# Rope's turned half multiplied ahead of the rotation and summed in PSUM, with the order of a stage rearranged

## What is computed

```python
def _rope(t):
    t1, t2 = (t[..., :d // 2], t[..., d // 2:])
    rot = jnp.concatenate([-t2, t1], axis=-1)
    return t * cos + rot * sin
q = jax.nn.silu(x @ Wq); k = jax.nn.silu(x @ Wk); v = x @ Wv
q = _rope(q); k = _rope(k)
energy = jnp.einsum('bhnd,bhmd->bhnm', q, k) * mask
out = jnp.einsum('bhnm,bhmd->bhnd', energy, v)
```

## Time and profile before

| | |
|---|---|
| runs, us | 509.13, 513.08, 508.7 |
| median | 509.13 |
| the profiled execution, its own time | 512.64 |
| its span, first to last instruction | 510.7 |
| mean granted TensorE clock | 0.84 |
| busy in the span, PE / DVE / ACT / POOL | 367.9 / 267.4 / 204.7 / 290.5 |
| first energies of the stages 1 to 6 start at | 42.54, 72.84, 108.61, 141.52, 177.34, 207.56 |

### The profile page before, as it was taken

How to read it: one execution, slowest core, us unless ns; L and a number is a source line. 1 busy time by engine, 2 the same in 40 slices (tenths; PEclk the granted TensorE clock), 3 DMA queues, 4 the chain that set the end, 5 groups by cost and what they waited for, 6 DMA issues and landing times.

```text
span 510.7 us, 10114 instructions
## 1 busy us (share of the span) xinstructions
PE 367.9 (72%) x2456; PEld 301.0 (59%) x2457; DVE 267.4 (52%) x1094; ACT 204.7 (40%) x583; POOL 290.5 (57%) x205
## 2 busy tenths in 40 slices
PE   6586878998698776932218878989988989999000
PEld 4464756876576565722117656878877878878000
DVE  0344563877938858587205554444544444444035
ACT  1232052160240421402005656766767676766100
POOL 3000000038377085687865888888888888888523
PEclk9797877799967977555658999999999999999555
DMA  7999994003223753159546999999999989998894
GB/s 216 330 332 303 451 354 147 2 15 76 62 56 82 293 159 81 42 163 348 125 102 132 162 149 157 156 155 155 157 154 153 153 146 164 154 156 121 149 255 152
DMA packets 66303, 85.81 MB, mean 168 GB/s; under 512 B 16840, under 2 KB 61302, under 8 KB 65894
## 3 DMA queue, kind: packets, MB, share of 16 engines
q1 hardware_dynamic: 35734, 59.82, 37.5%
q0 software_dynamic: 29680, 24.95, 33.7%
q10 hardware_dynamic: 864, 0.73, 0.5%
HBM read 45.86 MB, written 39.47 MB: 167 GB/s over the span
## 4 chain that ended last, share of the span: by engine, by line
DVE 23%; PE 21%; issue 17%; DMA 15%; POOL 10%; ACT 8%; ACTq 3%; SPq 1%; DVEq 0%; POOLq 0%
DMA sums_d<-e_sb,tok 10%; POOL rows_d L376 7%; PE B L413 5%; PE B L658 3%; ACT UPW L803 3%; POOL sums_d L391 3%; PE B L667 3%; PE B L486 2%; DVE e_sb L977 2%; ACTq L269 2%; DMA W<-sums_d 2%; ACT e_sb L823 2%; DVE stats L846 2%; PE B L570 1%; DVE h L1143 1%
## 5 line engine op out<-in xcount | busy, mean ns | idle before, releaser
L391 POOL DMA_INDIRECT sums_d<-e_sb,tok x112 | 174.0, 1554 | 41.9 <-issue 24.4
L376 POOL DMA_INDIRECT rows_d<-xrow,slot x77 | 104.1, 1351 | 156.4 <-issue 126.9
L658 PEld LDWEIGHTS B<-e_sb,UPW 128*128 128x128 f32 x796 | 105.6, 193 | 10.9 <-issue 5.0
L658 PE MATMUL B<-e_sb,UPW 128*128 128x128 f32 x796 | 109.9, 279 | 0.1
L667 PE MATMUL B<-W,e_sb 128*128 x224 | 74.4, 414 | 21.4 <-DVE e_sb L1134 11.1
L1134 DVE TENSOR_TENSOR e_sb<-e_sb,B 128x128 f32<-128x128 f32 (+1 forms) x112 | 32.3, 288 | 84.2 <-ACT e_sb L811 47.9
L803 ACT COPY UPW<-W 128x512 f32 (+1 forms) x112 | 63.2, 564 | 18.7 <-issue 18.7
L646 PE MATMUL B<-ident,e_sb 128*128 128x128 f32 x224 | 44.1, 280 | 19.9 <-DMA e_sb<-rows_d 19.2
L1118 DVE COPY e_sb<-B 128x256 f32<-128x256 f32 x112 | 46.9, 419 | 19.0 <-PE B L646 18.2
L667 PEld LDWEIGHTS B<-W,e_sb 128*128 128x128 f32 x224 | 34.0, 191 | 35.9 <-issue 35.6
L823 ACT ACTIVATE e_sb<-B,wcol 128x256 f32<-128x256 f32 x112 | 53.0, 473 | 0.0
(11 more groups left out here) (160 smaller groups left out, 475.3 us busy)
## 6 DMA issues: line engine op xcount, KB each, us to landing
e_sb<-rows_d SPq DMA_DIRECT2D x112, 152.5 KB
rows_d<-padrow SPq DMA_DIRECT2D x1, 7320.0 KB, 33.6
W<-in_wx SPq DMA_DIRECT2D x1, 7027.0 KB, 50.3
sums_d<-padrow SPq DMA_DIRECT2D x4, 1408.0 KB, 21.7
W<-in_wx SPq DMA_DIRECT2D x1, 4781.0 KB, 16.6
W<-in_wx SPq DMA_DIRECT2D x1, 4576.0 KB
W<-in_pt SPq DMA_DIRECT2D x4, 666.0 KB, 6.9
sums_d<-e_sb,tok POOLq DMA_INDIRECT x112
```

The costliest lines, as they stand in the source:

```text
L376: pool.indirect_dma_start(rows_d, bass.IndirectOffsetOnAxis(ap=slot[0:n, t, j:j + 1], axis=0), xrow[0:n, t, :], None).then_inc(done, 16)
L391: pool.indirect_dma_start(sums_d[c], bass.IndirectOffsetOnAxis(ap=tok[:, c:c + 1], axis=0), Y[:, c, :], None, compute_op=ALU.add).then_inc ...
L658: mm = pe.matmul(B[2 + u % 2][:, m * P:(m + 1) * P], UPW[:, u % 2, at:at + P], GT[:, u % 2, k, :], start=k == 0, stop=k == KC - 1)
```

## The change

Rope takes another form. VectorE now makes two products from q and k: times the cosine (`rp`) and times the sine with its sign (`rs`, a new buffer of 888 columns). PE turns `rs` and adds `rp` to it in the same PSUM bank through a matmul with the identity. ScalarE splits q and copies k out of PSUM.

The order of a stage changes. On PE the second tile's energies come ahead of the shared projection and no longer behind an embedding, and wait for the masks strip by strip; the first half of the embedding goes behind the attends; the rank comes ahead of the second half; in the first stages the projection and `fold` go ahead of the embedding. On VectorE `place` stands ahead of the embedding's moments and the norms, no longer behind rope. The ranks use bank B[1]. GpSimd scatters the last block's anchors ahead of three of tile 9's choices.

Small instructions of VectorE on one tensor and two constants become `scalar_tensor_tensor` with a tensor of constants, and moments and additions of a block's two tiles go in pairs.

```diff
-            for b, tiles in enumerate(BLOCKS):
+            half = CHOICES // 2 + 1
+            for b, tiles in enumerate(BLOCKS[:-1]):
                 pool.wait_ge(slot_ok, b + 1)
                 for t in tiles:
                     scatter(t, [0], scat_anchor)
                 for t in tiles:
-                    scatter(t, range(1, CHOICES), scat)
+                    scatter(t, range(1, half if t == NT - 2 else CHOICES), scat)
+            pool.wait_ge(slot_ok, NB)
+            scatter(NT - 1, [0], scat_anchor)
+            for t in (NT - 2, NT - 1):
+                scatter(t, range(half if t == NT - 2 else 1, CHOICES), scat)
...
             def rotate(b):
                 n = SIZES[b]
+                pe.wait_ge(rope_ok, b + 1)
                 for half in range(2):
-                    pe.wait_ge(qk_ok, 2 * b + half + 1)
                     for c in range(KC):
-                        m = pe.matmul(B[4 + half][:, c * BT:c * BT + n], turn[:, :], qk[:, half * KC + c, 0:n],
-                                      start=True, stop=True)
+                        part = B[4 + half][:, c * BT:c * BT + n]
+                        pe.matmul(part, turn[:, :], rs[:, half * KC + c, 0:n], start=True, stop=False)
+                        m = pe.matmul(part, ident[:, :], rp[:, half * KC + c, 0:n], start=False, stop=True)
                     m.then_inc(rot_ps, 1)
...
             def second_transposes(b):
                 pe.wait_ge(x2_ok, BLOCKS[b][-1] + 1)
+                if b:
+                    pe.wait_ge(slot_ok, b)
...
             def split_heads(b):
-                act.wait_ge(rope_ok, b + 1)
+                n = SIZES[b]
+                act.wait_ge(rot_ps, 2 * b + 1)
                 for odd in range(2):
-                    m = act.activation(q_two[:, odd, :, 0:SIZES[b]], qk[:, 0:KC, 0:SIZES[b]], ACT.Copy,
-                                       scale=parity[:, odd:odd + 1])
-                m.then_inc(qh_ok, 1)
+                    act.activation(q_two[:, odd, :, 0:n], two_chunks(B[4], n), ACT.Copy, scale=parity[:, odd:odd + 1])
+                act.wait_ge(rot_ps, 2 * b + 2)
+                act.copy(qk[:, KC:2 * KC, 0:n], two_chunks(B[5], n)).then_inc(qh_ok, 1)
...
-                step(dve.tensor_scalar(g2, g1, 2.0, -BIG, ALU.is_ge, ALU.mult))
+                step(dve.scalar_tensor_tensor(g2, g1, 2.0, least[0:n, 0:GROUPS * k], ALU.is_ge, ALU.mult))
...
             def rope(b):
                 n = SIZES[b]
                 dve.wait_ge(qk_ok, 2 * b + 2)
-                q, shape = of_images(qk[:, :, 0:n], b, 2 * KC)
-                r, _ = of_images(rp[:, :, 0:n], b, 2 * KC)
-                step(dve.tensor_tensor(r, q, cossin[:, 0, :].unsqueeze(1).unsqueeze(1).to_broadcast(shape), ALU.mult))
+                x, shape = of_images(qk[:, :, 0:n], b, 2 * KC)
+                for dst, factor in ((rp, 0), (rs, 1)):
+                    y, _ = of_images(dst[:, :, 0:n], b, 2 * KC)
+                    m = dve.tensor_tensor(y, x, cossin[:, factor, :].unsqueeze(1).unsqueeze(1).to_broadcast(shape), ALU.mult)
+                m.then_inc(rope_ok, 1)
                 add_bias(b)
-                for half in range(2):
-                    dve.wait_ge(rot_ps, 2 * b + half + 1)
-                    turned = B[4 + half][:, 0:KC * BT].rearrange("p (c t) -> p c t", c=KC)[:, :, 0:n]
-                    x, shape = of_images(turned, b, KC)
-                    dst, _ = of_images(qk[:, half * KC:(half + 1) * KC, 0:n], b, KC)
-                    m = dve.tensor_tensor(dst, x, cossin[:, 1, :].unsqueeze(1).unsqueeze(1).to_broadcast(shape), ALU.mult)
-                step(m)
-                dve.tensor_tensor(qk[:, :, 0:n], qk[:, :, 0:n], rp[:, :, 0:n], ALU.add).then_inc(rope_ok, 1)
-                dve.wait_ge(rope_ok, b + 1)
...
                 if mid is not None:
                     attended(mid)
+                if last is not None:
+                    place(last)
                 if coming is not None:
                     embedded(coming)
```

More of the change, by code:

```diff
@@ L602, in _ @@
                     normed_transposes(ahead)
+                for t in tiles[1:]:
+                    energies(mid, t)
+                if mid is not None:
+                    attend(mid, tiles[0])
                 if last is not None:
                     shared_up(last)
+                for t in tiles[1:]:
+                    attend(mid, t)
+                if ahead == 0:
+                    pe.wait_ge(ld["rest"], 16 * 12)
+                    project(ahead)
+                    fold()
                 if coming is not None:
                     embed(coming, 0)
[L607 to L610 removed]
                 if mid is not None:
                     out_project(mid)
+                if last is not None:
+                    rank(last)
                 if coming is not None and len(BLOCKS[coming]) > 1:
                     embed(coming, 1)
[L615 to L617 removed]
+                if ahead is not None and ahead > 0:
                     project(ahead)
[L619 to L622 removed]
                 if ahead is not None:
@@ L1008, in attended @@
                 dve.wait_ge(h2_ok, BLOCKS[b][-1] + 1)
-                for t in BLOCKS[b]:
-                    stat(h[0:TILES[t], t, :], t, b, 1)
+                moments(b, 1)
             def shared_mult(b):
@@ L1063, in _ @@
                 if last is not None:
-                    place(last)
                     shared_add(last)
```

78 lines of the change are left out of this document (37 added, 41 removed).

## The result

The changed kernel takes 523.43 us (median of 4, 522.26 to 525.62); the kernel before took 511.11 beside it on the same chip (median of 4, 508.7 to 515.48). The ratio is 1.024, with a 95% interval of 1.015 to 1.032: **slower by some 12 us**, where I had forecast 510.2 and a range up to 518. The profiled execution took 525.62 us with a span of 523.8, 13.1 more than the span of before. In what follows spans are compared with spans, and changes of the total by ratios.

A forecast was written before the change was run, and what follows sets the result against it. The last anchor scatter, gating part two, was taken as the bound. Start of the fifth stage +8.9, next stage +0.5, slots -3.3 and scatters -5.0 gave +1.1 us on 509.13: 510.2, range 501 to 518.

The forecast's parts named there:

- What bounds it: Whole run: the last block's anchor scatter lets part two start, and the 251.2 us from there are fixed.
- the anchor's landing: Hinge between the two parts: SP's first table entry follows the last anchor scatter's issue by 5.56 us, as before.
- The prologue: Before the first stage: projection and fold ahead of the second embedding bring the first rope at 41.9, +4.6 us.
- Rope and rotations: End of each stage: eight rotations on the path take 5.1 us; rope to next energies 10.4 us against 5.3.
- The energies themselves then run at full level: Start of each stage: the clock falls in the rotations, recovers there, and the energies run at full level.
- the stages' miss: Five stages, from first energies to the sixth's: the forecast sum had them change by -0.4 us.
- the reordering's term: Within a stage: second energies and attends moved forward bring the product 3.3 us earlier, 7.7 us in, at full level.
- the place's gain: Last block's scatters: three of tile 9 move behind the anchor's, which was to win 5.0 us.
- Slots: Last stage: slots, which came 22.5 us in before, were to come 3.3 us sooner.
- My three terms for the slots: Last stage: norms no longer ahead -2.4, routing's small instructions -1.5, low-level shared projection +0.7; carried as -3.3 us.
- The routing's small forms: VectorE's routing in the last stage: replacement instructions cost 162 ns each, -1.5 us.
- the rotation runs low throughout: Rival: rotations and gate at the low clock, and the prologue lowered too; +10.1 us, 519; chance 0.24.
- The third: Rival: the early anchor buys nothing, as GpSimd is late or the table unready; 5.0 us return, 515; chance 0.06.

The follow-up runs named there:

- x1: Changed kernel with the second embedding put back ahead of the projection and the fold in the first stages; 515.96 us, ratio 1.003 to the kernel before.
- x7: Changed kernel with the second tile's energies and the attends back behind the shared projection and the embedding's first half; 525.14 us, ratio 1.026 to the kernel before.
- x4: Changed kernel with the last block's anchor scatter back behind all 14 scatters of block 4; 524.60 us, ratio 1.024 to the kernel before.
- x2: Changed kernel with gate, shared output and second transposes moved ahead of the rotations on TensorE; 500.60 us, ratio 0.977 to the kernel before.
- x11: Changed kernel with x1's and x2's changes together, and `place` put back behind rope on VectorE; 500.28 us, ratio 0.977 to the kernel before.
- x5: Changed kernel with the last weight load issued behind the wait for the anchors' scatters; 529.60 us, ratio 1.030 to the kernel before.

## Why the prediction was wrong, step by step

**What bounds it** held. The run hinges on the anchor's landing, and the part behind it was 249.4 us from SP's first load against 250.2.

**The prologue**: forecast 41.9 for rope, up to 43.6 with a fall of the clock; measured 43.51. The projection began at 21.34 rather than 20.3, and its first part ran at the low level (5.52 us, 3.16 in x1). I had given the whole projection 7.2 us, 1.5 more than the 5.7 of the earlier trace rows, without saying for what; it took 8.1, and the embedding began at 33.2 rather than 31.4. The mechanism was right, the size 1.6 us short, and x1 confirmed the mechanism. Part of the 1.6 is spread: the eight kernels with this prologue reached rope at 42.8 to 44.9.

**Rope and rotations**: the eight rotations took 4.9 to 6.0 us up to the gate (forecast 5.1), and rope to energies 10.50, 10.11, 11.30, 10.12 and 10.96 (10.4). Right within 0.9.

**The failed step** is "The energies themselves then run at full level", and with it the product 7.7 us into a stage. I let the level fall once in a stage, at the rotations, and saw that it recovers by the gate; I did not ask what comes behind the recovery. In the first and second stages ScalarE's split left a second gap of 2.09 and 1.56 us, and the energies after it ran low; the shared output, which takes 1.1 us between gate and energies in the later stages, is not yet in the list there. In the fifth the level fell under the second tile's energies (195.49, 3.10 us) behind a rotation that had been low to 190. Product after energies was 9.26, 10.02, 7.88, 7.86 and 10.99 against a forecast of 7.5 to 7.7: 7.7 us more in five stages, which is all of the stages' miss of 7.9 but 0.2 (the other pieces, up to 1 us each way, cancel). The pieces that were at the full level came out at 7.9, so the reordering's term was right; in the stage compared, x7 showed that 1.7 us of it went to the clock at the next wait.

**The second failure** is the anchor's landing, which I took over as 5.56 us from the kernel before. I noted the larger weight load "well ahead". But the load goes out 16.0 us later than before (241.77) and the anchor, with fewer scatters ahead of it, only 8.6: 20.8 us lie between them and not 28.2, and the scatter comes 3.1 us behind the load's end. +5.6 us, and with x4 the place's gain is 0.4 instead of 5.0.

**Slots** came 17.2 us into the last stage (243.7), 2.0 better than forecast: the product came 5.95 us in, where it was 7.70 before and I had added 0.7. (My three terms for the slots add up to -3.2, not the -3.3 that I carried on.) The routing's small forms took what I had put down for them: L910 in place of L893 reads

```profile
L910 DVE SCALAR_TENSOR_TENSOR gs<-gs,least x6: 162/166/169, 100.1 to 250.9; 111x8 f32<-111x8 f32 x5, 111x4 f32<-111x4 f32 x1
```

This includes the one at 234.93, beside a scatter that ran from 234.09 to 235.45. The Trainium skill's page "SBUF — State Buffer", section "Who interferes with whom", has a VectorE instruction with two SBUF inputs, as this form is, contend with a GpSimd instruction that reads SBUF. Beside the scatters the trace shows no such delay (169 ns at most); whether a scatter's instruction is of the kind that the page means, no run here shows.

In sum: prologue 1.7, stages 7.9, slots -2.0, landing 5.2, rest -0.8 make 12.0, the difference between +13.1 and +1.1. **The rivals**: the second, "the rotation runs low throughout", came nearest with 519, but not by its mechanism; the rotations had the price of my forecast, and the low level showed at energies, routing and projection. The third had the early anchor buy nothing, and it bought 0.4 us, but for another reason, the landing. GpSimd did meet the first adds late, at 286.11 where their rows were ready at 284.47, and the part behind SP's first load was none the longer for it (249.4 us against 250.2).

## What to carry to other kernels

Work put on the path behind a long wait is paid twice: by its duration, and by the clock to which TensorE falls in the wait. So order an in-order engine's list such that what is ready, and above all what other engines wait for, stands ahead of what must wait; here that was worth 4.6% of the run (x2; 3.2 of its 26.1 us lie in the anchor's landing), and shortening the path to the wait without filling it was worth nothing in the total (x7). When a transfer's landing is taken over from an old trace, check what other transfer is in the queue at the new time: a few us nearer to a 5 MB load doubled it, from 5.56 to 11.13 us. And when work is moved, see who waits for its semaphore: in x11 the rotations did.

## What the hardware showed that I had not expected

- Eight products without use ahead of each wait made the changed kernel 1.8% faster; the granted clock was 1.00 through the rotations that had run at 0.50.
- The level can fall while TensorE is busy: in the changed kernel it was 1.00 at 193.48 and the energies from 195.49 took 3.10 us against 2.03 in the stage before, behind only 0.67 us of idle but with a low stretch to 190. The granted clock was 0.50 from 198.6 to 203, with TensorE busy without a gap.
- An indirect scatter of 74 rows landed in 5.6 to 6.1 us when issued 8 us or more behind a weight load's end, or with no load near, and in 6.8 to 11.7 us within 5 us of that end; in the stretch beside the load, at 244 to 249, scatters took 13.2 to 13.9.
- With the anchor in its early place GpSimd's third scatter behind it started 0.8 us after the anchor had landed, in every kernel that had this order (273.71 and 274.51 in the changed one, 268.54 and 269.35 in x5). With the old order there was no such pause. What holds it there is open. It cost nothing that shows: the first add came 11.7 us behind SP's first load, against 12.8 before.
